# A merged instruction order laid out anew for a four-layer adaLN kernel

## What is computed

```
h = layernorm(x) * (1 + ca) + sa ;  x = x + ga * attn(h)
h = layernorm(x) * (1 + cb) + sb ;  x = x + gb * ffn(h)
```

```
L0A  causal softmax attention, tanh output
L0F  mixture of 8 experts, top 2 of them, iterated twice, gelu
L1A  block-wise linear attention, 8 heads, blocks of 32 tokens
L1F  grouped mixture of 8 experts (SwiGLU)
L2A  retention: rotated q and k, decay per head, group norm
L2F  mixture of 16 experts, top 2
L3A  state space layer: h = exp(dt*A)*h + dt*B*x, y = sum over 16 states of C*h
L3F  mixture of 8 experts, top 2, tokens gathered by expert
```

## Time and profile before

| | |
|---|---|
| three runs | 1228.77 us median, 1224.02 to 1233.12 |
| the profiled execution | 1225.84 us, its span 1223.8 us |
| granted TensorE clock, mean | 0.926 |
| PE, DVE, ACT, POOL busy | 1082.9, 872.7, 685.5, 493.8 us |
| instructions | 18281 |

### The profile page before, as it was taken

The page is one execution under the profiler, slowest core; times in us unless marked ns, Lnnn a source line. Parts: engine busy times, 40 slices in busy tenths (PEclk is TensorE's granted clock), DMA queues, the critical chain, the costliest instruction groups (busy, mean ns, idle before and its releaser), DMA issues.

```text
span 1223.8 us, 18281 instructions
## 1 busy us (share of the span) xinstructions
PE 1082.9 (88%) x6855; PEld 654.4 (53%) x6855; DVE 872.7 (71%) x2050; ACT 685.5 (56%) x1155; POOL 493.8 (40%) x475
## 2 busy tenths in 40 slices
PE   7999999899999899999999867779899987659978
PEld 5766544344444354456444313464568676338868
DVE  4745547567666768788799899675686989966446
ACT  4477566686745586655676724562525786544221
POOL 2014122212213520184246456525455465686363
PEclk9999999999999789999999868769799998869989
DMA  8103000000000000000000000000514043147583
GB/s 257 57 9 138 1 1 0 1 1 2 1 1 18 1 2 1 20 1 1 18 1 1 0 0 1 1 3 33 172 52 166 33 164 112 33 168 232 209 291 92
DMA packets 36071, 70.14 MB, mean 57 GB/s; under 512 B 3088, under 2 KB 26128, under 8 KB 35472
## 3 DMA queue, kind: packets, MB, share of 16 engines
q0 software_dynamic: 9680, 45.88, 10.6%
q1 hardware_dynamic: 26304, 23.10, 6.0%
HBM read 59.34 MB, written 9.63 MB: 56 GB/s over the span
## 4 chain that ended last, share of the span: by engine, by line
PE 60%; DVE 14%; POOL 8%; ACT 8%; issue 6%; DMA 2%; another core or an unknown queue 1%; DVEq 0%; SPq 0%; POOLq 0%; ACTq 0%
PE ps L899 9%; PE ps L2177 5%; PE ps L1477 5%; PE ps L2185 3%; DVE own L2035 2%; PE ps L861 2%; PE ps L673 2%; PE ps L1276 2%; PE ps L1751 1%; PE ps L659 1%; POOL own L2059 1%; POOL own L1721 1%; PE ps L1455 1%; PE ps L1754 1%
## 5 line engine op out<-in xcount | busy, mean ns | idle before, releaser
L899 PE MATMUL ps<-own,g_f 128*128 128x512 f32 x320 | 147.8, 602 | 0.1
L899 PEld LDWEIGHTS ps<-own,g_f 128*128 128x128 f32 x320 | 59.2, 191 | 67.2 <-issue 61.0
L1226 POOL TENSOR_TENSOR own<-own 128x512 f32<-128x512 f32 x32 | 40.1, 1254 | 131.1 <-PE ps L899 95.5
L2035 DVE TENSOR_TENSOR_SCAN own<-own,carry 128x512 f32<-128x512 f32 x48 | 77.7, 1618 | 15.5 <-POOL own L2059 13.6
L2059 POOL TENSOR_TENSOR own<-own 128x512 f32<-128x512 f32 x32 | 50.7, 1585 | 53.2 <-ACT own L1985 53.0
L1939 PE MATMUL ps<-own,g_c 128*128 128x512 f32 x64 | 44.5, 784 | 30.5 <-POOL own L2065 30.4
L1976 ACT ACTIVATE own<-own,Acol 128x512 f32<-128x512 f32 x64 | 45.2, 714 | 40.1 <-PE ps L1939 38.9
L1895 POOL TENSOR_TENSOR own<-own 128x512 f32<-128x512 f32 x32 | 44.5, 1392 | 55.7 <-DVE own L1869 35.9
L1477 PE MATMUL ps<-g_l,own 128*128 128x512 f32 x128 | 59.5, 611 | 7.7 <-issue 7.3
L531 ACT ACTIVATE own<-xs,sm 128x128 f32<-128x128 f32 x128 | 52.5, 483 | 24.0 <-POOL sm L523 24.0
L2399 DVE TENSOR_TENSOR own<-ps,own 128x512 f32<-128x512 f32 x53 | 36.1, 682 | 41.4 <-PE ps L2177 13.3
(11 more groups left out here) (498 smaller groups left out, 2984.7 us busy)
## 6 DMA issues: line engine op xcount, KB each, us to landing
so<-own SPq DMA_DIRECT2D x10, 256.0 KB
g_l<-p_l SPq DMA_DIRECT2D x1, 2449.0 KB, 13.4
own<-sx SPq DMA_DIRECT2D x9, 256.0 KB, 9.5
g_f<-p_f SPq DMA_DIRECT2D x1, 2223.5 KB, 10.6
own<-cs SPq DMA_DIRECT2D x8, 256.0 KB, 3.4
sx<-brow SPq DMA_DIRECT2D x2, 960.0 KB, 12.4
g_l<-p_l SPq DMA_DIRECT2D x1, 1866.0 KB, 7.9
sx<-brow SPq DMA_DIRECT2D x1, 1472.0 KB, 14.3
```

The lines of the kernel that those rows point to most:

```text
L899: x = e.matmul(s.bank["V%d%d%d" % (it, k, cc)][:, :], ew2[:, m, 128 * cc:128 * cc + 128], gm, start=False, stop=m == 3)
L2035: e.tensor_tensor_scan(H, A, H, init, ALU.mult, ALU.add).then_inc(*s.dve.up("H%d" % n))
```

## The change

Only the string `ORDER` changes. It has the same length, and the same number of each letter; no instruction is added, removed or altered. The string was made with another assumption than before: that an instruction of DVE on SBUF and one of POOL on SBUF exclude each other in time.

```
 ORDER = (
-    "ttyyyojkkokpopepplpfooooaolaqnfqlfmaqqafnmgasfraaraakkkeqksnmkkkffsksrksirrkafdfaaaaiofohddkkakaeefkkffkiicoahaaoocchjhd"
...
+    "yotykkjootppklppfeoolpanqqfnaamassssimaffqraaraaoqgdoerrkkklmoqsryfhkinooddkkkkkdfkfieooidiacaeofonahaafaoddkaffaaakkkcc"
...
 )
```

More of the change, by code:

```diff
@@ new lines @@
+    "farkhkllaalkdfakffkfakdnnddngnfaabiaggfnnllikkkbkgbbkgafaffafaaafbbfdlfktkdgkddikkdddkikaakafkadpqnnfdninddnnlcialadkaad"
+    "dkanaalnnaqqkdhqiiaapdffnaqgnkddefddfaaiaaanfninndkdpofdkaaakkipakfpbgdiididddnddnnndnodfffnfniddnnkodikdkdidkdikdiikaaa"
+    "dddfaafanfknafiifdktddkkaaaiapfkfaafakfafdfdidaaniasafaapfanaaafnqqlafnsfsbbbsaskakkkibpgkkbgggbbgbgkkbgllaglllbbglllblf"
+    "flbfbgbggaaaagaafpgfakgllaalpkkallkkdlbbbkbblflbblbfblbblbbkgqggbffblfqbbkkggpkiblbbkqbbbkggbkglbqbgbkkllalalagqfaffaafa"
@@ new lines @@
+    "ggkkkgfaakckccmgkclhrrpclplcchhhhlcphlhpcflbhbbagfccagmmbgfagammmlkbbhfkcgfmmaaffmmmpbfflfclhclhhcffbbbkhlfhbkffbbkkfkhb"
+    "mqmmgbmlgggccgcmccgmchchmchmbbchaamafmgamcccrccffcfffmaahkffkkaaafcckfkkkfaffrcffmfkaffkackkcfcccffhrchmkhaakccfkkkhaamf"
+    "ffhrcmmfamffrffkbfakkaakbkkkhaahbbbkhbbbggqabhgklagkmmaqlbbklbkkkkllalbblfbalmbbbqmggkmbggkmklqgccmbblchhppllhppbfllgcga"
+    "cclgcfhamhakmagkfkmaqkakcccgkflkfakkmkchkklcclfllrcfkkfmckkkkalhhhlahhlakbbgbgbgbbbglbfccclfalgkckbaakcccrclhhhllccqqqqa"
@@ new lines @@
+    "gbhamkgkkkkkkahamkkakkkkkkbkqlakkkakkkkkbkgkkbkkckkgggmmlmbbgggggggmmcclkkkrcpplmpccccuupccrlflcgmphaglfcchhghaafakkahkr"
+    "akaakakkcfkpkmfmpahkabkbgmfmgagkpfampfgmhahkhprbfkkhagmampbmafgpmfbgglgbgakpagkfakfpfmgbbbllapmplmamckclllflhpchhackbgkk"
+    "cckhgcgkkmgbmmlbllggflhcbcmlbblglgngbggmdlgblgbkgbkddssggllglbdglmgllrrlaribbbrhdllbbddlldiiidlilflnnibangbnniilrddlchld"
+    "hqkkqicckqqgccppphnnnnndpdfbdhmmgibiiafllbbihlllilpblgagllglklbkilndgbklllbgngbklkllbflnbgkngldldkbbkkdnlnbklibllllllnch"
@@ new lines @@
+    "cnbhlhllsblmhmhhbhlmhmbhlmlbllllcllhhlhllclhhcllhlkhlclmhhmmhmchmcammhccldmiddhilcldlhnlnchcmhhammhhcvvmhhcdqqqqmmmddhmn"
+    "agdfddqlcihkkifkkckhkhdhcsnmhddmmhhmhhachkccmcdmmnfmbasgcmfcbbmclcbiimmgbmlblambblilbmblgallcihiqcmklggqaapmabdllqbbgkgm"
+    "qbklqfafrarlklgqarkbkapfbkagrqhbklablflgfqkafaapakgqkabfpkbfbgaqgakaqlchpbagqaakkfbflddddkkllafpclldlkmmgmkahlscaflapmcn"
+    "hammmddhkkkcfmncmbagnmmbpdlmlanhkcnhcmmmhmcmmcmhlscmhimiqqccicmmkckmqqgmmmcimmnqncmnmcmpmmmmbcngmmpppnfbnlbmndmmldcmmmmd"
@@ L72 @@
+    "cchmkcschswccssimrmckkkckdhriccdmmmnncnchimccnnrcnsncndrhmwmnnmnncccchnrncmcnncnhcssnurccmmnchnmmsncccdndnihddddniisicmn"
+    "ncccdndsimmwddididnhnnccndddddiiimdnmnncsdndiddididsnmnndndiddididnnssssndswddidisrxdnrdddisdnnnixdddxsnndirdnddrsidndnn"
+    "rnnrndddddrddiirdndnnddddinndniddddndnidddnndidnxsssndsmddsdidsssnmdmnmdnmdnndwnnnnx"
 )
```

57 lines of the change are left out of this document (19 added, 38 removed).

## The result

The changed kernel took 1271.24 us (median of 4 runs, 1269.65 to 1271.66), the kernel before beside it 1230.43 (1224.02 to 1233.12): a ratio of 1.0329, 95% interval 1.0300 to 1.0358. The forecast was 1214, the range ended at 1241, and slower had a chance of 0.19.

The account below looks back on a forecast made before the run. PE was taken as the bound up to 600 us, DVE and POOL from 600 to 800 and 1000 to 1100. 1225.8 - 12 - 1.5 = 1212.3 us, 2.9 more for the median, 1 less for clock: 1214, range 1190 to 1241.

Parts of the forecast that it names:

- Up to 600 us the matmuls are the bound and an order can win little.: First 600 us: PE is busy for 568 of 600 us, so no time was expected to come or go there.
- What the new order assumes is a real effect of this trace, and the old order was evidently not made for it.: Whole run: DVE and POOL exclude each other for some SBUF instructions, and the old order lets both start together.
- 21 us pulled apart, 9 given back, sum -12.: DVE and POOL on the chain: 21 us of known collisions separated, 9 us lost to 36 new neighbours, 12 us won.
- The chain's excess: Time of DVE and POOL pieces on the chain of waits over their forms' shortest instructions: 52 us in 61 pieces.
- pairs within six letters: Colliding partners near each other in the string: 47 pairs (39 us) in the old, 22 (18 us) in the new.
- PE's clock, -1 us: Where PE idles less, at clocks 0.85 and 0.81, it may be granted more clock, worth 1 us.
- the two stretches that I watched: From 600 to 800 and 1000 to 1100 us, where DVE and POOL were said to set the pace.
- The tail, -1.5 us: Chunk 2's last send 2.5 us earlier, with one more gather ahead costing 1.0 us: -1.5 us.
- Rival 3: Slower: assumption too wide, POOL's products put later than needed, in L3A of chunks 0, 1 and 3; 1241.5 us, chance 0.17.
- Rival 1: Order wins much more: the two DVE-bound stretches close up and PE's clock comes back; middle 1197 us, chance 0.18.

Follow-up runs that it names:

- thin_after: The changed kernel with five of POOL's long product and sum lines cut to 8 of 512 columns, waits and signals left: 0.9860 of the kernel before.
- thin_before: The kernel before with the same five POOL lines cut to 8 of 512 columns, waits and signals left: 0.9633 of the kernel before.
- none: Two strings laid out by search from two random starts, assuming DVE and POOL never exclude each other: 1.6 and 0.9% behind those with the wide assumption.
- s34: The kernel before with the new string from letter 2360 (620 us) to the end: ratio 1.0015 to the kernel before.
- repair: The changed kernel with its string altered only between letters 1470 and 2360, by moves of at most 12 places: ratio 1.0300 to the kernel before.
- s3: The kernel before with the new string only in letters 2360 to 3180 (about 620 to 850 us): 1208.20 us beside 1217.19 of the kernel before.
- s4: The kernel before with the new string only from letter 3180 (850 us) to the end: +0.6% against the kernel before.
- opt_wide: String laid out anew by search from s3's, POOL excluding every DVE instruction with all operands in SBUF: 1207.38 us beside 1218.49 of the kernel before.
- s1: The kernel before with the new string only up to letter 1470 (413 us): ratio 1.0058 to the kernel before.
- s2: The kernel before with the new string only in letters 1470 to 2360 (413 to about 620 us): +1.8% against the kernel before.

## Why the prediction was wrong, step by step

**"Up to 600 us the matmuls are the bound and an order can win little."** This is the step that failed. It is right as written and I used it for both signs, setting the change there to 0. Where PE is busy for 568 of 600 us PE's standing leaves an order at most 32 us to win, while a stop at a queue's head finds hardly any cover, so it can lose more easily than win: 27 us were lost by 600 us, 16.4 of them PE standing and 10.7 PE busy for longer. thin_after shows that most of the loss remains without POOL's long instructions. The forecast named this as what would sink it, and so it was.

**"What the new order assumes is a real effect of this trace, and the old order was evidently not made for it."** The first half holds: the lay-outs with the assumption have 43 to 52 us less lengthening than those without, and thin_before, though it also spares POOL work, gained 44 us. The second half was inferred and is wrong in its consequence: the new string has 147 us of lengthening, the old one 142, so neither is better in this, while "none", which truly ignores it, has 158 to 160.

**21 us pulled apart, 9 given back, sum -12.** The chain's excess went from 52 to 45 us, -7, so sign and size of this term were fair. That such a sum on the chain turns into time one for one was assumed; the time went the other way. The count of pairs within six letters said nothing of the rest of the path, which is the larger part: the order string also sets what ACT and PE wait for, and I costed none of that. The term missing from the sum is "stops at the heads of the queues of PE and ACT", which I had at nothing. Over the whole run PE stands 26.6 us longer, 16.4 of them by 600 us, and is busy 18.6 us longer at the lower clock.

**PE's clock, -1 us.** Wrong in sign: the clock fell where PE had more gaps, from 0.95 to 0.92 in 350 to 600 us, though it rose to 0.90 and 0.93 in the two stretches that I watched.

**The tail, -1.5 us.** PE's delay grows by about 10 us after 1175. The sends were moved as described. Why the tail is longer is open: the send and the load in its chain stand in the chain of s34 too, and repair, with the same string there, grows by only 3.3 us.

**Rival 3** had the right side and the wrong mechanism. It put the loss into L3A and into line 1939's wait, above 30 us; that wait fell to 21.6 us, and the stretch of its place is the one where the new string is better. POOL's idle time before line 1895 did rise, for another reason:

```profile
L1895 POOL TENSOR_TENSOR own<-own 128x512 f32<-128x512 f32 x32 | 44.2, 1381 | 66.4 <-DVE own L1869 57.5
```

55.7 us became 66.4, behind DVE. In the stop at 542.89 one sees how: L1869 stands behind L1435 in DVE's queue, and POOL's L1895 waits 1.31 us for it. **Rival 1** had a true core: s3 alone gives -0.7%, and its delay of -12 us at 750 us comes where I had put the gain. It doesn't last there: -3.3 us at 825. The trace of before held both the place of the gain and the room for the loss; the chance of 0.19 for slower weighed only collisions.

## What to carry to other kernels

A new order of fixed queues is a change of every wait, not only of the ones it was laid out for: cost what it can lose in the stretches where the bounding engine is nearly full, since there nothing covers a stop, and read the heads of that engine's queue in old and new order. A stretch where an engine is the bound is where an order can win least and lose most. A planner's assumption may be right and its string still worse: lay strings out with and without it by the same means and from more than one start, all on one chip; here two starts on two chips lay 0.7 to 2.6% apart. Compare traces only if the kernel before has one from the same chip. Taking the new order stretch by stretch found a version better than both at once.

## What the runs showed of the hardware

- Collisions follow the lay-out in a way that can be steered: 106 to 160 us of lengthening for the same instructions.
- An activation table load took 1.28 us each time, and the place where a foreign step stands in ACT's queue decides on it: 126 loads before, 129 after, 134 and 138 in the two strings of "none", 124 to 125 in s34, s3 and s4. The one at 442.00 lay in front of what PE waited for.
- The mean granted clock goes with PE's idle time only roughly. The changed kernel has 0.915 with 167.5 us idle, before 0.926 with 140.9, s3 0.933 with 130.9. But opt_wide, with the least idle time of the kernels that do all the work, 122.9 us, also has 0.926.
- In the traces of three of the five sets engines stand for something that the profile doesn't name: ACT for 21.3 us in that of before, PE for 7.26 us at 855. In the traces of the other two sets there are no such waits, and the delays of s1 and s2 show the one at 855 us at 6 us. The cause is open.
